# Criss-cross attention on one core: scales per block of four image rows instead of a pass over each image, work items of 128 pixels, and another dealing of the items

## The reference

```python
q = jnp.einsum('bchw,oc->bohw', x, Wq) + bq[None, :, None, None]   # 64 channels
k = jnp.einsum('bchw,oc->bohw', x, Wk) + bk[None, :, None, None]   # 64 channels
v = jnp.einsum('bchw,oc->bohw', x, Wv) + bv[None, :, None, None]   # 512 channels
eH = jnp.einsum('bchw,bcpw->bhwp', q, k)          # along the column
eH = jnp.where(diag, -jnp.inf, eH)
eW = jnp.einsum('bchw,bchp->bhwp', q, k)          # along the row
att = jax.nn.softmax(jnp.concatenate([eH, eW], axis=3), axis=3)
attH, attW = att[..., :H], att[..., H:]
outH = jnp.einsum('bcpw,bhwp->bchw', v, attH)
outW = jnp.einsum('bchp,bhwp->bchw', v, attW)
return gamma.reshape(()) * (outH + outW) + x
```

## Time and profile before

| | |
|---|---|
| Median of 3 runs | 4430.83 us |
| The profiled execution's own time | 4432.19 us |
| Its span, first to last instruction | 4430.4 us |
| Busy: PE, PE weight loads, DVE, ACT, POOL | 3546.2, 2449.1, 2561.2, 1878.5, 1221.3 us |
| Granted TensorE clock, mean of the span | 0.859 |
| DMA | 1179.38 MB, mean 266 GB/s |
| Prologue, up to the start of the loop | 322.7 us |
| One iteration of the loop (7 of them) | about 533.8 us |
| Attention of image 7 alone | 370.9 us |

### The profile page before, as it was taken

How to read it: one execution, slowest core, us unless ns; L and a number is a source line. 1 busy time by engine, 2 the same in 40 slices (tenths; PEclk the granted TensorE clock), 3 DMA queues, 4 the chain that set the end, 5 groups by cost and what they waited for, 6 DMA issues and landing times.

```text
span 4430.4 us, 97049 instructions
## 1 busy us (share of the span) xinstructions
PE 3546.2 (80%) x33624; PEld 2449.1 (55%) x33624; DVE 2561.2 (58%) x3802; ACT 1878.5 (42%) x3852; POOL 1221.3 (28%) x1075
## 2 busy tenths in 40 slices
PE   3987888778887887878878788877888788884865
PEld 1544665446654564645655466554665446653765
DVE  6546665466553864548655476555665466653743
ACT  2535634166342752427533374325644156341611
POOL 0010151402513034220343214331152402513253
PEclk9998799888998798987999879989799887997666
DMA  7958598986999769996899968899598996999399
GB/s 282 295 186 270 179 291 265 315 286 183 324 266 329 258 198 304 294 316 217 234 298 297 309 209 254 275 319 297 180 286 266 326 287 181 311 268 301 94 293 303
DMA packets 824053, 1179.38 MB, mean 266 GB/s; under 512 B 56560, under 2 KB 574192, under 8 KB 823536
## 3 DMA queue, kind: packets, MB, share of 16 engines
q1 hardware_dynamic: 509136, 831.94, 61.4%
q10 hardware_dynamic: 314400, 340.86, 24.1%
HBM read 832.83 MB, written 339.74 MB: 265 GB/s over the span
## 4 chain that ended last, share of the span: by engine, by line
issue 36%; DMA 25%; PE 22%; POOL 8%; DVE 3%; SPq 2%; ACT 2%; ACTq 1%; POOLq 0%; DVEq 0%
DMA xr<-x 21%; PE banks L1032 4%; PE banks L1033 4%; PE banks L1034 4%; POOL acc L496 4%; DMA v_in<-v_pixel_major 3%; PE banks L1106 3%; PE banks L1108 2%; PE banks L1107 2%; POOL prob_col L486 2%; POOL qk_pair L468 2%; PE banks L1084 1%; SPq L377 1%; DVE x_lo L803 1%; ACT v_out L590 1%
## 5 line engine op out<-in xcount | busy, mean ns | idle before, releaser
L1032 PE MATMUL banks<-wv_hi,x_hi 128*128 128x512 f16 x2304 | 930.1, 404 | 235.9 <-DVE x_lo L803 235.8
L811 DVE SCALAR_TENSOR_TENSOR v_out<-banks,proj,v_out 128x512 f16<-128x512 f32 x576 | 431.3, 749 | 1031.6 <-ACT v_out L590 1031.3
L496 POOL TENSOR_TENSOR acc<-acc,xr 128x768 f32<-128x768 f32 x384 | 714.5, 1864 | 815.9 <-DMA xr<-x 741.9
L1033 PE MATMUL banks<-wv_lo,x_hi 128*128 128x512 f16 x2304 | 924.2, 401 | 0.0
L1034 PE MATMUL banks<-wv_hi,x_lo 128*128 128x512 f16 x2304 | 919.8, 399 | 0.0
L468 POOL TENSOR_TENSOR qk_pair<-qk_f,qk_pair 128x256 f16<-128x256 f32 x288 | 196.3, 681 | 2125.8 <-ACT qk_pair L606 2117.8
L590 ACT ACTIVATE v_out<-banks,proj 128x512 f16<-128x512 f32 x576 | 391.2, 684 | 888.4 <-PE banks L1034 882.4
L1106 PE MATMUL banks<-prob_row,v_in 96*128 96x96 f16 x3072 | 490.2, 221 | 199.1 <-DMA v_in<-v_pixel_major 185.3
L892 DVE SCALAR_TENSOR_TENSOR acc<-banks,att,acc 128x384 f32<-128x384 f32 x768 | 443.9, 609 | 195.4 <-PE banks L1108 194.4
L1032 PEld LDWEIGHTS banks<-wv_hi,x_hi 128*128 128x128 f16 x2304 | 236.5, 103 | 505.7 <-issue 299.6
L1108 PE MATMUL banks<-prob_row,v_in 96*128 96x96 f16 x3072 | 489.5, 221 | 0.0
(11 more groups left out here) (104 smaller groups left out, 7029.4 us busy)
## 6 DMA issues: line engine op xcount, KB each, us to landing
v_in<-v_pixel_major SPq DMA_DIRECT2D x768, 384.0 KB, 7.3
x_raw<-x ACTq DMA_DIRECT2D x290, 512.0 KB, 7.2
x_next<-x SPq DMA_DIRECT2D x384, 384.0 KB, 3.7
v_pixel_major<-v_out ACTq DMA_DIRECT2D x576, 256.0 KB, 4.0
xr<-x SPq DMA_DIRECT2D x384, 384.0 KB, 9.5
out<-acc SPq DMA_DIRECT2D x384, 384.0 KB, 8.4
qk_halves<-qk_pair ACTq DMA_DIRECT2D x288, 128.0 KB, 4.1
x_first<-x SPq DMA_DIRECT2D x24, 768.0 KB, 8.2
```

What stands on the lines that cost most here:

```text
L496: nc.gpsimd.tensor_tensor(acc[tt][:, px], acc[tt][:, px], xr[n % XR][:, :], ALU.add).then_inc(res_added, 1)
L811: nc.vector.scalar_tensor_tensor(out=v_out[tile % V_OUT][:, :, 1, :], in0=bank[tile % 2][:, :].rearrange("p (t c) -> p t c", t=CT), scalar ...
L1032: nc.tensor.matmul(dst, s_hi, m_hi, start=(t == 0), stop=False)
L1033: nc.tensor.matmul(dst, s_hi, m_lo, start=False, stop=False)
```

## The change

The largest value of an image gives way to a bound for each block of four image rows. The block has 384 pixels (`BLK = G * W`) and three items, each a tile of 128 pixels with its V matmuls (12 of 512 columns, as before) and its own QK matmuls (12 of 128 columns). There are 72 items to an image.

- `squares` (ACT, in the item with sub 1) squares the next block's `x_raw` in two instructions of 128x768 with a running sum. PE sums over the partitions with two one-column matmuls on `ones` (`block_bound`, sub 2), DVE makes the scales in a chain of small instructions (`block_scales`, sub 2). The two `proj` buffers alternate.
- `x_raw` has still two buffers, now of 768 KB. `x_hi` and `x_lo` have three buffers of 128 pixels (`SL`). `qk_pair` has one buffer instead of two, and `low_qk` moves from POOL to DVE.
- As q and k of one image now carry 24 scales, POOL brings them to one (`to_common_scale`, 72 instructions of 128x384 in float16, before the score pairs). Row pairs wait for their blocks' share of it, and a load of q and k has a semaphore for each piece. The V scales go into the factor with which the transposed probabilities are split (`part_scale`), which costs no instruction. `image_scales` makes these numbers in 8 small DVE instructions.
- Gone are `load_next`, `x_first`, `see_next`, `see_all`, `reduce_xmax`, `make_scales`, `use_scales` and the wait of an image's first split for them.
- The residual comes in chunks of 192 KB, one for each group, in four buffers (`XR` = 4), and the first four are asked for in the middle of the column stretch.
- The dealing: HEAD 12 items, one with each row pair, one with each second column pair, STATS 4, 10 to a column stretch, 6 to a row stretch, TURN 6.
- POOL normalises two groups ahead for each one attended, and holds no items.

```diff
-    BLK = 256
+    G = 4
+    BLK = G * W
     PT = BLK // P
     NB = HW // BLK
-    SUBS = PT + 1
-    ITEMS = NB * SUBS
+    ITEMS = NB * PT
+    SL = 3
...
-    XR = 3
+    XR = 4
...
-    HEAD = 20
-    STATS = 6
-    TURN = 10
+    HEAD = 12
+    STATS = 4
+    TURN = 6
+    COL_DEAL, ROW_DEAL = 10, 6
...
             def load_block(m, n):
 
-                act.wait_ge(x_split, m * NB + n - 2 + SPLIT0 + 1)
+                act.wait_ge(x_split, m * ITEMS + (n - 1) * PT + SPLIT0)
...
+            def squares(m, n):
+
+                act.wait_ge(x_loaded[n % 2], m * (ROUNDS["x"] * 16) + (n // 2 + 1) * 16)
+                act.wait_ge(bound_mm, m * NB + n + ONE0)
+                act.wait_ge(qk_ready, m * NB + n - 1 + QK_READY0)
+                for s in range(2):
+                    if s:
+                        act.wait_ge(sq_ready, 2 * (m * NB + n) + 1)
+                    nc.scalar.activation(
+                        qk_f32[:, :].bitcast(BF16).rearrange("p (t c) -> p t c", t=2),
+                        x_raw[n % 2][:, 2 * s:2 * s + 2, :], ACT.Square, accum_out=x_sq[:, s:s + 1],
+                    ).then_inc(sq_ready, 1)
...
             def item(m, i):
-                n, sub = divmod(i, SUBS)
-                if sub == 0:
-                    if n > 0:
-                        high_qk(m, n - 1)
-                    if n + 1 < NB:
-                        split_hi(m, n + 1)
-                if sub < PT:
-                    high_v(m, n, sub)
...
+                n, sub = divmod(i, PT)
+                if sub == 0 and n > 0:
+                    high_qk(m, n - 1)
+                split_hi(m + (i + 1) // ITEMS, (i + 1) % ITEMS)
+                if sub == 1:
+                    squares(m + (n + 1) // NB, (n + 1) % NB)
+                if sub == 2:
+                    load_block(m + (n + 2) // NB, (n + 2) % NB)
+                high_v(m, i)
+                if i > 0:
+                    store_v(m, i - 1)
...
+            def block_bound(m, n):
+                pe.wait_ge(sq_ready, 2 * (m * NB + n + 1))
+                nc.tensor.matmul(bank[2][:, BLK:BLK + 1], ones[:, :], x_sq[:, 0:1], start=True, stop=False)
+                nc.tensor.matmul(bank[2][:, BLK:BLK + 1], ones[:, :], x_sq[:, 1:2], start=False, stop=True).then_inc(
+                    bound_mm, 1
+                )
...
+            def to_common_scale(b, n):
+
+                piece = n * QK_PIECES // NB
+                if n == 0:
+                    wait_alone(pool, att_ready, b + 1)
+                if n == 0 or piece != (n - 1) * QK_PIECES // NB:
+                    wait_alone(pool, qk_loaded[piece], (b + 1) * 96)
+                px = slice(n * BLK, (n + 1) * BLK)
+                for a in (q_both, k_hi, k_lo):
+                    nc.gpsimd.tensor_scalar(
+                        a[:, px], a[:, px], att[:, COMP_QK + n:COMP_QK + n + 1], None, ALU.mult
+                    ).then_inc(qk_common, 1)
...
             def score_pair(b, p):
                 o, q = pair_at(p)
                 if p == 0:
                     wait_alone(pe, row_added, b * (GROUPS // 2) + ONE0)
-                    wait_alone(pe, qk_loaded[0], (b + 1) * (QK_PIECES // 2 * 96))
-                if p == NP // 2:
-                    wait_alone(pe, qk_loaded[1], (b + 1) * (QK_PIECES // 2 * 96))
+                if o == ROW:
+                    wait_alone(pe, qk_common, 3 * (b * NB + 2 * (p + 1)))
```

571 lines of the change are left out of this document (244 added, 327 removed).

## The result

The changed kernel takes 4616.29 us (median of four runs, 4606.03 to 4621.13) against 4427.9 us (four runs, 4410.83 to 4435.36): a ratio of 1.0408, with a 95% interval of 1.0378 to 1.0437. It is 4% slower; the forecast was 4270 us, 3.6% faster. The profiled execution spans 4619.3 us, 188.9 more than before.

What follows compares the result with a forecast made beforehand. No engine was taken as full throughout: DMA bounds HEAD and row 1, DVE and ACT are busiest in row pairs. From 4432.2, -42, -2, -112 (seven iterations of -16) and -5 gave 4271, 4270 on the median's scale; range 4130 to 4440.

Steps and rivals of the forecast that it cites:

- The start (-42, -2): Prologue: first matmul at about 26 us instead of 68.45, -42; the rest 252 us instead of 254, -2.
- The removed waits (-22.1 an iteration): Three PE waits in each iteration disappear: 7.4 at the image border, 8.3 for POOL's normalisation, 6.4 for `qk_f`.
- -7.4 and -2 predicted: Image border: PE's wait for `x_lo` goes, -7.4; a row stretch gains from less DMA work, -2.
- -6.4, +3 and -2 predicted: Row 1 and TURN: PE's wait for `qk_f` goes, -6.4; `x_raw` landings in TURN, +3; row stretch, -2.
- the chain of `xr`: Row stretches: four loads in flight, a group costs (landing + 0.95 + 0.9)/4; as a slower rival, 4590 us, 10%.
- HEAD (0): HEAD: about 55 of 56 us, with `x_raw` landings of 10 us; 0, ends -6 and +8.
- The row pairs (+7, ends 0 and +25): Row pairs: VectorE's busy time goes from 42.4 to 49 us, at the present 86% 56 instead of 49.
- POOL's scalings (0): 72 scalings of q and k at 0.6 us each, 43 us, covered by HEAD and the row pairs: 0.
- -5: Last image: q and k used piece by piece and POOL free of the other half, 5 us less.
- The column pairs (0): Column pairs: six tiles replace twelve chunks, 13.8 us on DVE against 10.4, hidden by the score loop and PE's clock.
- DVE and ACT fill the pairs: Rival in the pairs: +25 for +7, total 4396 us; chance 10%.
- the rival of the weight loads: QK matmuls of 128 columns paced by weight loads, 0.106 us for 0.054, 45 us an image: 4630 us; chance 2%.

Runs made afterwards that it cites:

- e3: The changed kernel with the six tiles of the column pairs dealt to the row stretches (nine each instead of six): 4496.96 us, ratio 1.0149.
- e2: The changed kernel with POOL scaling only 8 columns of each 384 of q and k: 4522.08 us, ratio 1.0204.
- e1: The changed kernel with PE and ScalarE doing a pair's tile ahead of its scores and exponentials, block scales moved ahead on VectorE: 4639.3 us, ratio 1.045.
- e4: The changed kernel with tile first on PE and ScalarE, and POOL's scalings cut to 8 columns: 4553.72 us (median of three), ratio 1.0259.
- e9: The changed kernel with ScalarE alone doing the tile ahead of the pair's exponentials: 4534.61 us, ratio 1.0235.
- e11: The changed kernel with ScalarE's tile ahead of its exponentials and POOL's scalings cut to 8 of 384 columns: 4385.96 us, ratio 0.9887.
- e10: The changed kernel with ScalarE's tile first, no tiles in column pairs, and the last image's scalings shared by POOL, VectorE and ScalarE: 4397.03 us, ratio 0.9924.

## Why the prediction was wrong

**The start (-42, -2): right.** The first matmul starts at 25.21 and the loop at 279.1, 43.6 earlier.

**The removed waits (-22.1 an iteration): right in place.** Column 1 is 8.3 shorter, the very wait for POOL's normalisation; the border lies in a stretch that is 10.5 shorter (-7.4 and -2 predicted), row 1 with TURN is 15.1 shorter (-6.4, +3 and -2 predicted). The row stretches' gain was bigger than forecast. e3 prices a tile there at 1.65 us, so four fewer make 6.6 of it. `xr` lands in 6.5 in row 1, and the chain of `xr` as the prediction counted it, (6.5 + 0.95 + 0.9) / 4 a group, would make a stretch of 100; it takes 85. PE's waits there are for `v_in` (18.2 us). Whether DMA at a share of 1.06 or the chain of `xr` in the same SP queue makes them was not tried.

**HEAD (0): right**, -3.3. The `x_raw` landing is 9.9 us there for the 10 assumed.

**The row pairs (+7, ends 0 and +25): wrong, +30.9.** The failing step is "at the present 86% that is 56 instead of 49". The sum of VectorE's work was fair (49 predicted; 54.3 measured in the changed kernel, 49.9 where POOL does not scale), and so was the 86%, but only as the rate of a stretch in which VectorE is the bound. (The prediction's window of 49 us left out the end of the row pairs; the whole of them takes 52.5, with VectorE busy 45.2, again 86%. And 49 at 86% are 57, so the term by its own working is +8.) The change brought two other chains. The alternation takes 6.4 to 7.4 us a pair (6.8 in the mean of an iteration of e2, where POOL hardly works, and 7.1 in the changed kernel), and it is what set the pace. POOL's scalings take 7.6 a pair, with their head start, and set the pace once the alternation is gone. Their row pairs in a table of four, all measured:

```
                          POOL scales all   POOL scales 8 of 384
exponentials first              83.6               80.1
ScalarE's tile first            75.2               57.8
```

Taking away POOL's work gives 3.5, taking away the alternation 8.4, both 25.8. The order of the changed kernel makes the alternation. Before, ScalarE and PE had the item ahead of the pair's own work. These lines of the full diff turn it round, and I read them as neutral:

```diff
 # ScalarE; PE likewise, with score_pair
                 for p in range(PAIRS):
-                    if items and p < NP:
-                        item(b + 1, HEAD + p)
                     exp_pair(b, p)
...
+                    if items and item_at_pair(p) is not None:
+                        item(b + 1, item_at_pair(p))
```

But the order is not the whole of it. e1 has the old order on all three engines and takes 87.0, and 77.1 with POOL's work gone (e4): another chain, of PE and VectorE, and as long. What else differs from the kernel before is how far ahead the split stands: there `split_lo` of a block comes two items ahead of the first product that needs it, here one tile ahead, and in e1 PE waits 28.4 us for `x_lo` and VectorE 35.4 for PE's scores. That the shorter look-ahead is why the old order no longer serves is argued from the code and these waits; no run varied it. What is shown is that moving ScalarE's tile alone (e9, and e11 against e2) breaks the alternation: 22.3 us where POOL does not scale.

**POOL's scalings (0): wrong, as the text itself allowed.** "At over 1.2 us each they would come onto the path": they take 1.27. The bound of 0.93 had come from an add in f32 with two inputs, on the reasoning that one input and half the size can't take longer than half of it. They can. The Trainium skill, "GPSIMD Engine Reference", section 4.1 "Engine selection", calls instructions with one input roughly line-rate; this trace does not agree: POOL takes 1.27 for 384 elements of f16, and VectorE 0.41 for the same in e10's last image. In the loop it is the second chain, and in the last image, where no HEAD covers it, the first: the step "**-5**" for that image named POOL's freedom as a gain and came out at +74.6. When the scaling goes, 62 of them go, 50 in the row pairs. The other 13 lie in column 1, column 2 and row 2 of that image (5.4, 5.8 and 5.3 us longer in e2 than before, with HEAD 3.9 shorter), and no run explains them.

**The column pairs (0): wrong, +22.6.** The failing step is "hidden by the two-deep score loop and PE's higher clock". I had weighed VectorE there and not PE, which was busy 44.0 of 48.2 us before. The clock did rise (0.53 to 0.81), but the scores start every 0.16 us at either level, and a tile's first products run at the lower one. The scan's chunks had nearly been hidden there (2.9 us for twelve), the tiles cost 24.8.

**Column 2 (not in the sum): +4.9.** PE waits 3.3 us for evacuations in it where it waited 0.8 before. Ten whole tiles in place of fifteen smaller items leave four or five `attend`s in a row, with three output buffers; that this is the cause is argued from the waits, not tried. The matmuls of the bound (`block_bound`), which the prediction put at nothing there, take another 1.3. With the 34 us of seven iterations it is a tenth of the miss.

The sum of the misses: (30.9 - 7) x 7 = 167 for row pairs, 158 for column pairs, 80 for the last image, 34 for column 2 and 10 for the statistics, less 23 for HEAD and 76 for the row stretches and the border, are 350; 4616 - 4270 = 346. Of the rivals, "DVE and ACT fill the pairs" had the place and a third of the size. Of its signs, iterations of 505 to 525 us (556.4), pairs of 95 to 110 (154.6) and VectorE over 85% busy in the row half (66%) failed. The two falsifiers at the end (row stretches over 110, PE waiting over 8 a block in HEAD and TURN) did not come true: I had set them where I felt unsure, and not where the sum rested on a busy share.

## What to carry to other kernels

A busy share (86%) may be carried over to the changed kernel only if the waits of the engines for each other are the same. The order changes them, as where a diff swaps "item, then pair" for "pair, then item" on two of three engines; putting the old order back did not put the old pace back, so look as well at how far ahead each operand is made (argued above, not tried). Write out one round of the loop with its waits before anything is added up. Two chains of like pace hide each other: an experiment that removes one and gains nothing has not acquitted it, and only the table of four shows both. Before work is dealt into a stretch, look at the busy share of each engine there, PE's too, and price an unseen instruction by its own operation and type, not by another's rate.

## What was not expected of the hardware

- VectorE is slower while POOL works. In the row pairs of the changed kernel and of e2 (without the scaling), the same VectorE instruction:

```profile
L784 DVE SCALAR_TENSOR_TENSOR x_lo<-x_raw,proj,x_hi 128x512 f16<-128x512 f32 x12 | 10.4, 867 | 21.4 <-ACT x_hi L555 21.4
...
L845 DVE TENSOR_SCALAR nmax<-nmax,att 96x8 f32<-96x8 f32 x13 | 4.8, 372 | 0.5
```

```profile
L785 DVE SCALAR_TENSOR_TENSOR x_lo<-x_raw,proj,x_hi 128x512 f16<-128x512 f32 x11 | 8.3, 751 | 21.3 <-ACT x_hi L556 21.3
...
L846 DVE TENSOR_SCALAR nmax<-nmax,att 96x8 f32<-96x8 f32 x12 | 2.7, 229 | 0.4
```

  867 ns for 751, and 372 for 229: 4 us of VectorE's busy time in the row pairs (54.3 for 50.4).
- One multiplication of 128 x 384 in f16 by a scalar for each partition takes 1.27 us on POOL, 0.62 on ScalarE and 0.41 in the mean on VectorE (e10's last image: median 0.31, longest 0.64).
- A matmul whose operands step through memory by an image row costs 0.16 us for 96 columns, at 2.4 and at 1.2 GHz alike; with neighbours in memory it is 0.045 and 0.08. The clock does not set this pace, and PE's busy share does not tell it apart. That the reads set it is inferred from the step, and which operand's reads is not told.
- 128-column products with weights of their own start every 0.055 us (279.15, 279.20, 279.26 and 279.31 in the changed kernel), so the rival of the weight loads did not come about.
